# A two-layer sequence kernel on one core: who issues the first transfers, and where four small pieces of the start stand

## The chip, the cores and the metric

One core of a Trainium2 chip. The time is that of one execution on the device, in microseconds, from the first to the last instruction with what lies around them. The whole input lies in the chip's memory at the start and the whole output there at the end; the host only lays arrays out.

## The reference, cut to what matters

Two residual layers over x, 16 sequences of 256 steps with 512 channels each. The first is a causal convolution of 16 taps, one weight for each channel and tap. The taps are the rows of `cond`, which is also the first state of the second layer, a GRU:

```
x = x + conv(x, cond)                      # y[t] = sum over 16 taps, per channel
h = cond                                   # [16, 512]
for t in range(256):
    gi = x[t] @ W_ih + b_ih                # 512 -> 1536: r, z, n
    gh = h    @ W_hh + b_hh
    r = sigmoid(gi_r + gh_r);  z = sigmoid(gi_z + gh_z)
    n = tanh(gi_n + r * gh_n)
    h = (1 - z) * n + z * h
    out[t] = x[t] + h
```

All in float32.

## The kernel before

**Layout.** The 512 channels are 4 chunks (C = 4) over 128 partitions. The GRU's gates are computed in two halves, f = 0 and 1, each of two chunks (H = 2). The batch of 16 is the stationary side of a matmul: `recur(t, f, c)` (line 534) adds h's chunk c times W_hh to a PSUM tile `pg` for half f, in four column groups. `product(q)` (line 419) adds the input part x times W_ih for two steps at once, m = t // 2; q counts (m, f, c). A later scheme with formed weight differences (`group`, line 512) takes over from step 15.

**One step.** TensorE does the 64 recurrent matmuls of both halves; VectorE transposes the gates out of PSUM (lines 803, 807, 798), ScalarE does sigmoid and tanh (711, 713, 716), GpSimd z times h (408), VectorE the scans that give n's argument and h (815, 828). In the time between, TensorE does the products of coming steps.

**The convolution** is done in several ways. The first 16 steps: chunks 0 to 2 by VectorE as 60 multiply-adds (`first`, the first four steps, line 731, 12 of them; `rest`, line 741, 48 of them, the last 22 = LATE behind the two first transposes of the input gates), chunk 3 by TensorE with diagonal matrices that ScalarE writes (573, 696). Steps 16 to 47: chunk 0 by VectorE (`early`, line 775, 16 taps spread over the steps of EARLY), chunks 1 to 3 by TensorE as a product with a banded matrix (`turn`, line 565, in the step of ROUNDS), which reads windows of x (`xw`, line 241) and the band (`tz`, line 235, itself gathered from the taps that ScalarE has stored to memory, line 692). `spread` (789) brings the result to x1 in the step of TURNED. From step 48 on VectorE does all (759).

**The start, engine by engine**, each in program order:

- SP: cond, the first 16 steps of x (`xs`, 512 KB), four chunks of W_ih, four of W_hh (768 KB each, 6 KB for each partition), then waits for the third chunk of W_hh, then the window for `early`, the bands and windows step by step.
- ScalarE: b_ih, b_hh, then waits for GpSimd's `cpad` (the taps), stores them, writes 16 diagonals, copies the summed biases into six PSUM tiles (`seed`, 655), takes chunk 3's convolution out of PSUM, and copies a part of each chunk of W_hh (705).
- VectorE: two fills; waits for cond and copies it as h; waits for the biases, adds and transposes them (lines 840 to 851) to `bc`; waits for `xs`; then the 12 and 26 multiply-adds, the two transposes, the last 22.
- GpSimd: `eye`, `cpad`, fills; waits for `bc`; fills `tz` (321); then six small operations on `base`, `q21`, `q12`, `q22` and `delta` (322 to 327), needed first in step 11; then the loop over the steps.
- TensorE: zero products to open PSUM and six more (WARM); chunk 3's taps; the products of steps 0 to 3; waits for the two input transposes; then for each chunk c of W_hh the recurrent matmuls of step 0, behind chunk 0 the product (m = 2, c = 3), behind chunk 1 the product (m = 2, c = 0) (AHEAD), and behind chunk 0 two zero products (IDLE).

A DMA issued by SP runs on queue 1 and one by ScalarE on queue 10 of the same 16 DMA engines. In step 10 TensorE waits for the last tap of `early`, then opens the PSUM tile `stage` with a zero product (641), since `early` sums in that tile.

Of the kernel before, what the change touches and what calls it, by code (L numbers as in the profile page):

```python
# [10 lines left out]
J, C, D = 4, 4, 32  # L11
B, T, F = 16, 256, 512
# [7 lines left out]
TB = 16  # L20
# [10 lines left out]
FEW = 4  # L31
WARM = 6
LATE = 22
IDLE = {0: 2}
AHEAD = {0: 3, 1: 0}
M2 = T // 2
RZ, IN, END = CH * D, 3 * CH * D, 4 * CH * D
Q = 3
# [7 lines left out]
def build(nc, x, cond, w_ih, w_hh, b_ih, b_hh, out):  # L46
    assert J * D == P
    ctx = ExitStack()
    with ctx:
        def sb(name, shape, dt=F32):  # L50
            return ctx.enter_context(nc.sbuf_tensor(name, shape, dt))
# [4 lines left out]
        def sem(name):  # L56
            return ctx.enter_context(nc.semaphore(name))
# [5 lines left out]
        xs = sb("xs", [P, C, TB * B])  # L63
# [7 lines left out]
        cnd = sb("cnd", [P, C, B])  # L71
# [29 lines left out]
        s_cnd = sem("s_cnd")  # L101
        s_small = sem("s_small")
        s_xs = sem("s_xs")
# [17 lines left out]
        s_first = sem("s_first")  # L121
# [50 lines left out]
        def x1_of(c, a, b):  # L172

            return x1[:, c, a % KEEP * B:(a % KEEP + b - a) * B]

        def window(k):

            return xb[k % 2]

        def products(t):  # L180

            ahead = [(2 * H + f) * C + c for c in AHEAD.values() for f in range(H)]
            return [q for q in range(2 * H * C + C * t, 2 * H * C + C * (t + 1)) if q < H * C * M0 and q not in ahead]
# [10 lines left out]
            return range(total * min(max(t - a, 0), b - a) // (b - a), total * min(max(t + 1 - a, 0), b - a) // (b - a))  # L194


        ROUNDS = {1: 4, 2: 6, 3: 8}
        TURNED = {1: 5, 2: 7, 3: 9}
        EARLY = {1: 2, 2: 2, 3: 2, 4: 3, 6: 3, 8: 3, 10: 1}
        SPANS = [(a - W2 - 4, a - 4) for a, _ in LONG]  # L200
        BAND = {1: 0, 2: 2, 3: 4}
        WINDOWS = {1: (1, 3), 2: (3, 5), 3: (5, 7)}
# [2 lines left out]
        FIRST = [(lag, c) for lag in range(FEW) for c in range(C - 1)]  # L205
        REST = [(lag, c) for lag in range(K) for c in range(C - 1)]
# [22 lines left out]
        @block.sync  # L229
        def _(sp):  # L230
            def band(c, g):
                if c == BANDED[0] and g == 0:
                    sp.wait_ge(s_scr, 16)
                    sp.wait_ge(s_band, len(BANDED))
                sp.dma_start(tz[c][W2 * g:W2 * (g + 1), :, g * K:(g + 1) * K],  # L235
                             bass.AP(scratch, (g * C + c) * TAPS, [[1, W2], [G * C * TAPS, NQ], [1, K]])
                             ).then_inc(s_tz[c], 16)

            def load(c, q):
                i, g = divmod(q, G)  # L240
                sp.dma_start(xw[c][W2 * g:W2 * (g + 1), :, i, :],  # L241
                             x[:, c, TB * i * B:(TB * i + W2) * B].rearrange("(p e) (w b) -> e w p b", e=G, b=B)[g]
                             ).then_inc(s_xw[c], 16)

            def load_long(k, c, i):
                a, b = LONG[k]
                if i == c == k == 0:
                    sp.wait_ge(s_c3, 1)
                if i == c == 0 and k == 1:
                    sp.wait_ge(s_early, K)  # L250
                if i == 0 and k >= 2:
                    sp.wait_ge(s_long, LONGS * (k - 2) + W2 // C * 3 * (c + 1))
                n = (K - 1 + b - a) * B
                at, to = n * i // PIECES, n * (i + 1) // PIECES
                first = (a - K + 1) * B
                sp.dma_start(window(k)[:, c, at:to], x[:, c, first + at:first + to]).then_inc(s_xb[k][c], 16)

            def store(k, c):
                a, b = STORES[k]
                sp.wait_ge(s_o, b)  # L260
                sp.dma_start(out[:, c, a * B:b * B], x1_of(c, a, b)).then_inc(s_out[k], 16)

            sp.dma_start(cnd[:, :, :], cond).then_inc(s_cnd, 16)
            sp.dma_start(xs[:, :, :], x[:, :, 0:TB * B]).then_inc(s_xs, 16)
            for c in range(C):
                sp.dma_start(wih[:, c, :, :], w_ih[:, c, :, :]).then_inc(s_wih[c], 16)
            for c in range(C):
                sp.dma_start(whh[:, c, F:], w_hh[:, c, :]).then_inc(s_whh[c], 16)
            sp.wait_ge(s_whh[C - 2], 16)
            sp.dma_start(xb[1][:, 0, :], x[:, 0, B:(W2 + TB) * B]).then_inc(s_xe, 16)  # L270
            for t in range(T):
                sp.wait_ge(s_h[0], t + 1)
                for c in BANDED:
                    if t == BAND[c]:
                        for g in range(G):
                            band(c, g)
                    for q in share(2 * G, WINDOWS[c], t):
                        load(c, q)
                for k in range(len(LONG)):
                    for c in range(C):  # L280
                        for i in share(PIECES, arriving(k, c), t):
                            load_long(k, c, i)
                for k, (a, b) in enumerate(STORES[:NB - 1]):
                    for c in share(C, (b, b + C), t):
                        store(k, c)
                for k, (a, b) in enumerate(STORES[NB - 1:-1], NB - 1):
                    if b == t:
                        sp.wait_ge(s_o, b)
                        sp.dma_start(out[:, :, a * B:b * B], x1_of(slice(None), a, b)).then_inc(s_out[k], 16)
            a, b = STORES[-1]  # L290
            sp.wait_ge(s_o, b)
            sp.dma_start(out[:, :, a * B:b * B], x1_of(slice(None), a, b)).then_inc(s_out[len(STORES) - 1], 16)
            sp.wait_ge(s_o, T)
            sp.dma_start(out[:, 0:CH, (T - 1) * B:], x1_of(slice(0, CH), T - 1, T)).then_inc(s_fin[0], 16)
            sp.wait_ge(s_last, 1)
            sp.dma_start(out[:, CH:, (T - 1) * B:], x1_of(slice(CH, C), T - 1, T)).then_inc(s_fin[1], 16)
            for k in range(len(STORES)):
                sp.wait_ge(s_out[k], 16 * (C if k < NB - 1 else 1))
            for f in range(H):
                sp.wait_ge(s_fin[f], 16)  # L300

        @block.gpsimd
        def _(pool):
# [15 lines left out]
            pool.wait_ge(s_bc, H)  # L319
            for c in BANDED:  # L320
                pool.memset(tz[c][:, :, :], 0.0).then_inc(s_band, 1)
            pool.memset(base[:, END:], 0.0).then_inc(s_prep, 1)
            pool.tensor_copy(base[:, 0:END], bc[:, 0, :]).then_inc(s_prep, 1)
            pool.tensor_copy(q21[:, 0:RZ], bc[:, 0, 0:RZ]).then_inc(s_prep, 1)
# [93 lines left out]
        def _(pe):  # L418
            def product(q):

                m, f, c = q // (H * C), q // C % H, q % C
                if m < 2 and f == 0:
                    pe.wait_ge(s_wih[c], 16)
                if m < 2 and c < C - 1:
                    pe.wait_ge(s_first, len(FIRST))
                if c == (AHEAD[0] if m == 2 else 0):
                    pe.wait_ge(s_seed[f], m + 1)
                if FEW <= 2 * m and c == 0:
                    pe.wait_ge(s_first, len(FIRST) + len(REST))
                for j in range(J):  # L430
                    i = pe.matmul(pg[m % Q][f][D * j:D * (j + 1), RZ:END], x1_of(c, 2 * m, 2 * m + 2),  # L431
                                  wih[:, c, :, :].rearrange("p (g k) (j d) -> p j g k d", g=3, j=J)
                                  [:, j, :, f * CH:(f + 1) * CH],
                                  start=False, stop=True, skip_group_check=True)
                if c == (C - 2 if m == 2 else C - 1):
                    i.then_inc(s_gi[f], 1)
# [162 lines left out]
            for c in range(C):  # L599
# [3 lines left out]
                for f in range(H):  # L603
                    if c < C - 1:
                        recur(0, f, c)
                    else:
                        recur_first(f, c).then_inc(s_gh[f], 1)
                if c in AHEAD:
                    for f in range(H):
                        product((2 * H + f) * C + AHEAD[c])  # L610
                for _ in range(IDLE.get(c, 0)):
                    pe.matmul(pcv[0][:, :], zeros[:, 0:P], zeros[:, :], start=True, stop=True)
# [3 lines left out]
            for t in range(1, T):  # L616
                m = t // 2
# [14 lines left out]
                for c in range(C):  # L632
                    for q in products(t)[c:c + 1]:
                        product(q)
                    for e, at in ROUNDS.items():
                        for r in range(2 * c, 2 * c + 2):
# [10 lines left out]
        def _(act):  # L647
# [14 lines left out]
            def staged(t):  # L662
# [20 lines left out]
                if r == 3 and ready(g + 1):  # L683
# [2 lines left out]
                        act.wait_ge(s_prep, 6)  # L686
                    act.activation(stage[:, 0:END + IN], base[:, :], ACT.Copy).then_inc(s_base, 1)

            act.dma_start(bih[:, :], b_ih).then_inc(s_small, 16)
            act.dma_start(bhh[:, :], b_hh).then_inc(s_small, 16)  # L690
            act.wait_ge(s_cp, 3)
# [31 lines left out]
        def _(dve):  # L723
# [138 lines left out]
            for t in range(T):  # L862
# [12 lines left out]
                for k, i in tapped(t):  # L875
                    long(k, i, RIGHT)
                    long(k, i, WHOLE)
                for c, at in TURNED.items():
                    if t == at:
                        for q in range(NT):  # L880
                            spread(c, q)
                done = sum(n for at, n in EARLY.items() if at < t)
                for lag in range(done, done + EARLY.get(t, 0)):
                    early(lag)
# [35 lines left out]
```

## Time and profile before

| | |
|---|---|
| median of 3 runs | 993.23 us (992.36 to 993.47) |
| the profiled execution | 991.44 us |
| its span, first to last instruction | 989.7 us |
| TensorE busy | 976.7 us, 99% |
| VectorE busy | 892.7 us, 90% |
| ScalarE, GpSimd busy | 467.3 and 447.2 us |

Times in the profile count from the span's start. A matmul's busy time is modelled and overlaps its neighbours, so TensorE at 99% is not TensorE at its peak; the chain of waits says more. SPq and ACTq are the sequencers that issue DMAs.

### The profile page before, as it was taken

The page shows a single profiled execution, that of the slowest core. Times are in us where ns is not written, and L with a number is a line of the kernel's source. Part 1 is how long each engine was busy: PE and PEld are TensorE (multiplying, and loading weights), DVE is VectorE, ACT ScalarE, POOL GpSimd, SP SyncE. Part 2 cuts the span into 40 slices and gives each one's busy share as a digit, 9 for nine tenths or more (in the row PEclk, how much of TensorE's full clock was granted, in tenths as well). Part 3 has the DMA queues.
Part 4 walks back from the last instruction along what each step waited for, and adds up shares of the span by engine and source line. Part 5 has one row for each costly group of instructions (what it writes and reads, how often), then busy time and mean ns, then how long its engine had stood idle before and what let it go on. Part 6 is the DMA issues. An engine that isn't in the chain of part 4 may idle for free.

```text
span 989.7 us, 59526 instructions
## 1 busy us (share of the span) xinstructions
PE 976.7 (99%) x24833; PEld 784.4 (79%) x24833; DVE 892.7 (90%) x3075; ACT 467.3 (47%) x1996; POOL 447.2 (45%) x1222
## 2 busy tenths in 40 slices
PE   8999999999999999999999999999999999999996
PEld 6778887888888777788888888888888888888875
DVE  7879999999999999999999999999999988888565
ACT  5334444444444444444454444544444444444443
POOL 6544444444444444444444444444444444444442
PEclk9999999999999999999999999999999999999999
DMA  8721001010010101001010010101001010010000
GB/s 304 73 40 35 25 11 38 15 41 19 16 37 12 40 19 30 26 14 34 20 35 25 16 33 16 40 20 28 24 15 37 14 30 17 11 31 4 26 14 14
DMA packets 67006, 32.17 MB, mean 33 GB/s; under 512 B 44464, under 2 KB 65584, under 8 KB 66736
## 3 DMA queue, kind: packets, MB, share of 16 engines
q1 hardware_dynamic: 66304, 28.25, 11.1%
q8 instruction: 195, 3.19, 1.4%
q14 instruction: 75, 0.61, 0.2%
q10 hardware_dynamic: 432, 0.11, 0.0%
HBM read 19.86 MB, written 8.49 MB: 29 GB/s over the span
## 4 chain that ended last, share of the span: by engine, by line
PE 93%; SPq 1%; DVE 1%; issue 0%; DMA 0%; POOL 0%; ACT 0%; DVEq 0%; POOLq 0%
PE pg L537 65%; PE pcv L463 12%; PE pg L453 8%; PE pg L463 4%; PE pcv L453 4%; SPq L241 1%; SPq L235 0%; PE pg L431 0%; DMA xw<-x 0%; POOL nzh L408 0%; DVE hp L828 0%; ACT rz L711 0%; DVE gt L803 0%; DVE gn L807 0%; POOL wt L349 0%
## 5 line engine op out<-in xcount | busy, mean ns | idle before, releaser
L537 PE MATMUL pg<-whh,hp 128*32 128x192 f32 x16368 | 712.8, 326 | 4.5 <-DVE hp L828 4.1
L537 PEld LDWEIGHTS pg<-whh,hp 128*32 128x32 f32 x16368 | 527.7, 110 | 136.7 <-DVE hp L828 6.5
L759 DVE SCALAR_TENSOR_TENSOR pcv<-xb,cnd,pcv 128x256 f32<-128x256 f32 (+2 forms) x588 | 315.2, 536 | 6.9
L408 POOL TENSOR_TENSOR nzh<-rz,hp 128x32 f32<-128x32 f32 x512 | 158.0, 309 | 347.6 <-ACT rz L711 347.5
L711 ACT ACTIVATE rz<-gt 128x64 f32<-128x64 f32 x512 | 136.6, 267 | 342.3 <-DVE gt L803 314.6
L803 DVE STREAM_TRANSPOSE gt<-pg 128x128 f32<-128x128 f32 x512 | 162.3, 317 | 51.7 <-PE pg L537 42.0
L828 DVE TENSOR_TENSOR_SCAN hp<-zcp,nzh 128x96 f32<-128x96 f32 x512 | 173.3, 338 | 11.9 <-ACT nzh L716 9.4
L716 ACT ACTIVATE nzh<-an 128x32 f32<-128x32 f32 x512 | 121.4, 237 | 127.3 <-DVE an L815 127.3
L815 DVE TENSOR_TENSOR_SCAN an<-rz,gn 128x64 f32<-128x64 f32 x512 | 149.9, 293 | 18.9 <-issue 0.4
L463 PE MATMUL pcv<-wt,sx 128*32 128x192 f32 x2880 | 150.0, 326 | 0.0
L713 ACT ACTIVATE zcp<-gt 128x32 f32<-128x32 f32 x512 | 110.9, 217 | 0.0
L807 DVE STREAM_TRANSPOSE gn<-pg 128x64 f32<-128x64 f32 x512 | 107.4, 210 | 0.0
L463 PEld LDWEIGHTS pcv<-wt,sx 128*32 128x32 f32 x2880 | 90.7, 110 | 19.6
L660 ACT ACTIVATE pg<-q 128x256 f32<-128x256 f32 x180 | 68.9, 383 | 36.5 <-POOL q L393 36.5
L334 POOL TENSOR_TENSOR x<-x,hp 128x64 f32<-128x64 f32 x255 | 81.4, 319 | 0.2
L453 PE MATMUL pg<-wih,x 128*32 128x96 f32 (+1 forms) x1440 | 61.3, 273 | 0.0
L463 PE MATMUL pg<-wt,x 128*32 128x96 f32 (+1 forms) x1440 | 61.3, 273 | 0.0
L463 PEld LDWEIGHTS pg<-wt,x 128*32 128x32 f32 x1440 | 46.7, 110 | 11.7
L393 POOL TENSOR_TENSOR q<-e,delta 128x192 f32<-128x192 f32 x60 | 35.8, 596 | 40.7 <-DVE hp L828 40.7
L798 DVE STREAM_TRANSPOSE gn<-pg 128x64 f32<-128x64 f32 x256 | 53.6, 209 | 0.0
L453 PE MATMUL pcv<-wih,x 128*32 128x192 f32 x960 | 50.0, 326 | 0.0
L453 PE MATMUL pg<-wih,sx 128*32 128x192 f32 x960 | 50.0, 326 | 0.0
(81 smaller groups left out, 552.1 us busy)
## 6 DMA issues: line engine op xcount, KB each, us to landing
xb<-x SPq DMA_DIRECT2D x96, 94.0 KB, 2.0
out<-x SPq DMA_DIRECT2D x60, 128.0 KB, 1.8
wih<-w_ih SPq DMA_DIRECT2D x4, 768.0 KB, 8.0
whh<-w_hh SPq DMA_DIRECT2D x4, 768.0 KB, 14.1
xw<-x SPq DMA_DIRECT2D x24, 64.0 KB, 3.4
xb<-x SPq DMA_DIRECT2D x16, 62.0 KB, 1.9
tz<-taps SPq DMA_DIRECT2D x12, 64.0 KB, 3.3
xs<-x SPq DMA_DIRECT2D x1, 512.0 KB, 4.6
```

The source lines that it names most:

```text
L408: pool.tensor_tensor(nzh[:, f, ::2, :, 1], chunks(rz[:, f, 1, :, 1]), h_of(t - 1, slice(f * CH, (f + 1) * CH)), ALU.mult).then_inc(s_zh[f], 1)
L453: i = pe.matmul(out[D * j:D * (j + 1), at:at + IN].rearrange("p (g k d) -> p g k d", g=3, d=D)[:, :, part, :], left, wih[:, c, :, :].rearr ...
L463: i = pe.matmul(out[D * j:D * (j + 1), at:at + IN].rearrange("p (g k d) -> p g k d", g=3, d=D)[:, :, part, :], left, wt[:, n, c, :, :].rea ...
L537: i = pe.matmul(pg[t // 2 % Q][f][D * j:D * (j + 1), 0:IN], hp[:, t % 2, 2 * c + 1 - t % 2:2 * c + 3 - t % 2, :, 1].rearrange("p u b -> p ...
L711: act.activation(rz[:, f, :, :, 1].rearrange("p g (c b) -> p (g c) b", b=B), gt[:, f, :, u], ACT.Sigmoid).then_inc(s_rz[f], 1)
L713: act.activation(zcp[:, f, ::2, :, 1], gt[:, f, CH:, u], ACT.Sigmoid, scale=-1.0).then_inc(s_zc[f], 1)
L716: act.activation(nzh[:, f, ::2, :, 0], chunks(an[:, f, :, 1]), ACT.Tanh).then_inc(s_n[f], 1)
L759: dve.scalar_tensor_tensor(x1_of(c, a, b)[:, lo:hi] if lag == K - 1 else sums, xx[:, c, (K - 1 - lag) * B + lo:(K - 1 - lag) * B + hi], cn ...
L803: dve.transpose(gt[:, f, :, :].rearrange("p c r -> p (c r)"), pg[t // 2 % Q][f][:, RZ:IN]).then_inc(s_trz[f], 1)
L807: dve.transpose(gn[:, t // 2 % 2, :, f, :, :, 0].rearrange("p u c b -> p c u b"), pg[t // 2 % Q][f][:, 0:RZ]).then_inc(s_tn[f], 1)
L815: dve.tensor_tensor_scan(an[:, f].rearrange("p n s -> p (n s)"), rz[:, f, 0].rearrange("p n s -> p (n s)"), gn[:, t // 2 % 2, t % 2, f].re ...
L828: dve.tensor_tensor_scan(hp[:, (t + 1) % 2, a:a + n].rearrange("p c b s -> p (c b s)"), zcp[:, f, 0:n].rearrange("p c b s -> p (c b s)"), ...
```

## The change

Six edits. ScalarE issues cond, xs, b_ih, b_hh in this order at its start, and SP begins with the weights. The product (m = 2, c = 0) is no longer pulled into the prologue: it is done in the steps, and three zero products stand behind chunk 1. The wait for the seed follows it to the chunk that now comes first. Chunk 3's banded product goes from step 8 to 9, its `spread` from 9 to 10. The 16 taps of `early` end in step 9: two in step 8, two in 9. GpSimd's six small operations wait until VectorE has done all 60 multiply-adds of the first 16 steps.

```diff
-IDLE = {0: 2}
-AHEAD = {0: 3, 1: 0}
+IDLE = {0: 2, 1: 3}
+AHEAD = {0: 3}
...
-        ROUNDS = {1: 4, 2: 6, 3: 8}
-        TURNED = {1: 5, 2: 7, 3: 9}
-        EARLY = {1: 2, 2: 2, 3: 2, 4: 3, 6: 3, 8: 3, 10: 1}
+        ROUNDS = {1: 4, 2: 6, 3: 9}
+        TURNED = {1: 5, 2: 7, 3: 10}
+        EARLY = {1: 2, 2: 2, 3: 2, 4: 3, 6: 3, 8: 2, 9: 2}
...
-            sp.dma_start(cnd[:, :, :], cond).then_inc(s_cnd, 16)
-            sp.dma_start(xs[:, :, :], x[:, :, 0:TB * B]).then_inc(s_xs, 16)
             for c in range(C):
                 sp.dma_start(wih[:, c, :, :], w_ih[:, c, :, :]).then_inc(s_wih[c], 16)
...
             for c in BANDED:
                 pool.memset(tz[c][:, :, :], 0.0).then_inc(s_band, 1)
+            pool.wait_ge(s_first, len(FIRST) + len(REST))
             pool.memset(base[:, END:], 0.0).then_inc(s_prep, 1)
...
-                if c == (AHEAD[0] if m == 2 else 0):
+                if c == (C - 1 if m == 2 else 0):
                     pe.wait_ge(s_seed[f], m + 1)
...
+            act.dma_start(cnd[:, :, :], cond).then_inc(s_cnd, 16)
+            act.dma_start(xs[:, :, :], x[:, :, 0:TB * B]).then_inc(s_xs, 16)
             act.dma_start(bih[:, :], b_ih).then_inc(s_small, 16)
             act.dma_start(bhh[:, :], b_hh).then_inc(s_small, 16)
```

## Rows read from the trace of the kernel before

**Rows 1.** Page, part 4: the chain that ended last, shares by engine and line.

```profile
PE 93%; SPq 1%; DVE 1%; issue 0%; DMA 0%; POOL 0%; ACT 0%; DVEq 0%; POOLq 0%
PE pg L537 65%; PE pcv L463 12%; PE pg L453 8%; PE pg L463 4%; PE pcv L453 4%; SPq L241 1%; SPq L235 0%; PE pg L431 0%; DMA xw<-x 0%; POOL nzh L408 0%; DVE hp L828 0%; ACT rz L711 0%; DVE gt L803 0%; DVE gn L807 0%; POOL wt L349 0%
```

**Rows 2.** The chain in order of time, steps 8 to 10: start us, us, what.

```profile
54.07 3.37 DMA xw<-x
...
59.56 2.60 PE pg L537 x64
...
67.72 0.65 DVE x L775
```

**Rows 3.** Waits to 75 us: engine, tile, line, releaser: us, times, longest.

```profile
PE pcv L641 <- DVE x L775: 1.1, 1, 1.1
...
PEld pcv L565 <- DMA xw<-x: 0.8, 1, 0.8
```

**Rows 4.** Timeline, SP's DMA issues: start us, us, engine, line, operation, count.

```profile
0.80 0.40 SPq L263 DMA_DIRECT2D cnd<-cond  x1
1.25 0.67 SPq L264 DMA_DIRECT2D xs<-x  x1
1.97 2.52 SPq L266 DMA_DIRECT2D wih<-w_ih  x4
```

**Rows 5.** Timeline, ScalarE: the taps' store and the last part of W_hh.

```profile
3.31 0.33 ACTq L692 DMA_DIRECT2D taps<-cpad  x1
...
22.19 0.63 ACT L705 ACTIVATE whh<-whh 128x512 f32<-128x512 f32 x1 [1.18 <-DMA whh<-w_hh]
```

**Rows 6.** Timeline, VectorE to the first gate transpose; brackets: idle before, releaser.

```profile
2.98 0.17 DVE L841 COPY bcol<-bih 128x4 f32<-128x4 f32 x1
...
3.41 0.77 DVE L849 STREAM_TRANSPOSE bc<-bcol 128x256 f32<-128x256 f32 x2
5.89 0.68 DVE L731 SCALAR_TENSOR_TENSOR x<-xs,cnd 128x64 f32<-128x64 f32 x3 [1.71 <-DMA xs<-x]
...
16.17 0.51 DVE L798 STREAM_TRANSPOSE gn<-pg 128x64 f32<-128x64 f32 x2
16.59 4.78 DVE L741 SCALAR_TENSOR_TENSOR x<-xs,cnd,x 128x128 f32<-128x128 f32 x22
23.38 0.32 DVE L803 STREAM_TRANSPOSE gt<-pg 128x128 f32<-128x128 f32 x1 [2.01 <-PE pg L551]
```

**Rows 7.** Timeline, TensorE's matmuls to step 0.

```profile
3.79 2.77 PE L581 MATMUL pcv<-zeros 128*128 128x512 bf16 x6
...
16.82 0.83 PE L537 MATMUL pg<-whh,hp 128*32 128x192 f32 x16
...
18.24 0.60 PE L612 MATMUL pcv<-zeros 128*128 128x512 bf16 x2
...
21.43 0.86 PE L431 MATMUL pg<-wih,x 128*32 128x192 f32 x16 [1.32 <-DVE x L741]
22.10 0.83 PE L537 MATMUL pg<-whh,hp 128*32 128x192 f32 x16
```

**Rows 8.** Timeline, GpSimd's bias copies and its first product of step 0.

```profile
9.68 6.73 POOL L323 COPY base<-bc 128x256 f32<-128x256 f32 x1
...
16.98 0.63 POOL L327 TENSOR_TENSOR delta<-bc 128x192 f32<-128x192 f32 x1
24.13 0.31 POOL L408 TENSOR_TENSOR nzh<-rz,hp 128x32 f32<-128x32 f32 x1 [6.52 <-ACT rz L711]
```

**Rows 9.** DMA queues from 8.0 to 8.5 us: packets, MB, share of engines.

```profile
q1 hardware_dynamic: 30, 0.18, 94.5%
q10 hardware_dynamic: 30, 0.02, 13.5%
```

**Rows 10.** DMA issues to 75 us: line, count, KB, median us to landing.

```profile
xs<-x SPq DMA_DIRECT2D x1, 512.0 KB, 4.6
...
taps<-cpad ACTq DMA_DIRECT2D x1, 96.0 KB, 7.1
```

## The prediction

> **What bounds the kernel now.** I read the chain of waits first. TensorE carries 93% of it, and line 537 alone, the recurrence, has 65% [rows 1]. From the twelfth step on every step is TensorE work back to back, and the change touches nothing there. So it can act only in the first 75 us: the prologue up to the first gate transposes at 23.38 us [rows 6], and steps 8 to 11, where the chain leaves TensorE. There it goes through a landing of the banded windows and then through a VectorE tap [rows 2]. The wait table prices these: 0.8 us on the last landing before line 565, 1.1 us before the opening product of line 641 [rows 3]. In the prologue I read each engine's own row of the timeline. SP issues cond, then xs, then the eight weight transfers [rows 4]; ScalarE issues the two biases meanwhile, and they have landed by 2.98 us, when VectorE reads them [rows 6]. VectorE handles the biases before xs, then runs its taps without a gap from 5.89 to 21.37 us, with only the two input transposes in between, and then waits 2.01 us for TensorE [rows 6]. TensorE waits 1.3 us for those taps at 21.43 us [rows 7], and ScalarE receives the last weight chunk at 22.19 us [rows 5]. The prologue is a close race between weights, taps and TensorE; whichever comes 1 or 2 us late sets the end.
>
> **The late steps.** Chunk 3's product goes from step 8 to step 9. Its last window landed at 54.07 + 3.37 = 57.44 us [rows 2]; the recurrent matmuls of one step are 2.60 us [rows 2], so a step later TensorE reaches it over 2 us after that, and the 0.8 us wait goes [rows 3]; the same products cost the same one step later. What is late next is only TensorE itself. The early taps now finish in step 9 instead of step 10: as many in all, 16, but line 641 no longer waits 1.1 us for the last one [rows 2, 3]. The four transposes of chunk 3 take its place at the end of step 10, behind the h of that step, and nobody needs them before step 12. Together -1.9 us. SP's issue order for the windows is unchanged and follows h, so it moves along.
>
> **The moved product.** product(2, f, 0) leaves the prologue, and with it the 1.3 us wait [rows 7]; three zero products stand there instead, about 0.3 us each by the pair of 0.60 us [rows 7]. Two of its halves return in steps 0 and 1, 0.33 us each, where TensorE waits for h anyway: 0 to +0.3 us, taken as +0.1.
>
> **The DMA issues.** SP's first weight transfer moves from 1.97 to about 0.80 us, since 1.17 us of issuing go from ahead of it [rows 4]. ScalarE now issues cond at 0.8, xs at about 1.25 and the biases at about 1.9 and 2.4. The bytes are the same, so the last chunk can land at most some 1.2 us earlier. But xs used to be ahead of the weights on one queue. Now it is on the other queue, beside them. How the two queues share is the term that decides, and the trace has one case of it: the taps, 96 KB from ScalarE at 3.31 us [rows 5], took 7.1 us to land [rows 10] although nothing else was on their queue. In the half microsecond from 8.0 to 8.5 us each queue got exactly 30 packets, SP's with 0.18 MB, ScalarE's with 0.02 MB [rows 9]. So the engines take turns by packet, whatever its size: 16 engines x 0.5 us / 30 = 0.27 us for one small packet and the 6 KB weight packet that goes with it.
>
> xs is 128 rows x 4 runs of 1 KB, 32 packets for each engine. Each bias is 128 rows of 48 B, 8 for each engine. With three completion packets that makes 51 turns behind xs's first: 51 x 0.27 = 13.8 us, less about five turns that fall on SP's own completion packets (-1.3). Starting at about 2.7 us, xs lands near 12 and the biases near 15.5; cond's own turns and the late start that the taps show (their landing is 4 us over what 8 turns cost) can add 0 to 4 us. I take 16.5 us for the biases. Bounds: 3 us, if the small packets aren't held up at all; 20 us, when the weights run out.
>
> VectorE's program reads the biases before it waits for xs. From the first bias copy to the end of the transposes of line 849 is 1.2 us (2.98 to 4.18), so the first tap starts at 17.7 instead of 5.89 us: 11.8 us later. The two input transposes end at 28.5 instead of 16.68, the taps at 33.2 instead of 21.37 [rows 6]. TensorE may start the recurrence only after those transposes. From there it needs, by its old rows [rows 7]: 2.0 us to the end of the two zero products (16.82 to 18.84), 0.65 for chunk 1, 0.9 for three zero products, and 1.28 from 22.10 to the first transpose at 23.38. That is 4.85 us, so the first gates stand at 33.4 us: +10.0 us. The weights, in by about 21, no longer matter.
>
> **Bias copies behind the taps.** GpSimd's copy of the base took 6.73 us beside VectorE's taps; the operations from its end to the end of delta took 1.2 us (16.41 to 17.61) [rows 8]. Run alone after the last tap I put all six at 1.8 us, bounds 1.5 and 3. They end at 35.0 us. The first nzh product stood 0.75 us behind the first gate transpose (24.13 against 23.38) [rows 6, 8], so it would be due at 34.15 and is 0.85 us late; a little is absorbed by the tanh beside it. I take +0.7. If xs came as early as before, the same six would end at 23.2 us and cost nothing.
>
> **A rule against the row.** The row shows 30 to 30 packets at 0.18 to 0.02 MB [rows 9]. The Trainium skill, "DMA: Bandwidth & Descriptors", section "Queues, rings and completion order", says that each engine switches queues only at packet boundaries and that a packet may hold 9 to 17 descriptors; its section "SWDGE vs HWDGE vs iDMA" adds that a packet is preferably at most 4096 B. If that grouping held here, four 1 KB runs would go per turn, xs would need 8 turns, and a bias one. By the page xs would then land at about 6 us; by the row at 12. The row speaks against grouping, since grouped taps of 768 B would show several of them to one weight packet.
>
> **Sum.** +10.0 + 0.7 + 0.1 - 1.9 = +8.9 us. The profiled execution took 991.44 us for a span of 989.7 us; it would become 1000.3. The median of the runs is 993.23, 1.8 above the profiled one, so I forecast 1002.1, taken as 1002.
>
> **Rivals.**
> (A) The small packets get through, grouped as above or for another reason: xs and biases land by 6 to 7 us. For it: the biases, beside cond alone, were in by 2.98 us [rows 6]. Against it: the equal counts of [rows 9]. VectorE then starts at 7 to 8 us, 1.3 to 2 late, which its 2.01 us of waiting [rows 6] mostly covers, the last weights come about 1 us earlier, and the six GpSimd operations may cost up to 0.7. Prologue +0.4, late steps -1.9: 991.7, not slower. It decides as long as the biases land before about 8 us.
> (B) Sharing lies between: the biases land at 9 to 12 us. The shift of the first gates is then 2.6 to 5.6 us, plus 0.7, less 1.9: 994.6 to 997.6.
> (C) The forecast plus a slow TensorE. With xs at 12 us it idles 5 us and more twice, where its longest idle now is 1.3 us [rows 7]. The granted clock is listed as 1.0 throughout, the upper of its two levels (2.4 GHz), but six equal zero products took 2.77 us at 3.79 us, 0.46 each, and two took 0.60 at 18.24 [rows 7]. The 4.85 us path and step 0 behind it at up to twice the price: +2 to +6, so 1004 to 1008; I take 1006. The Trainium skill, "TensorE: Matmul & The Clock Gate", section "Part 1: The HAM clock gate", says an idle array falls from 2.4 to 1.2 GHz; no row here shows a fall after an idle stretch.
> (D) Everything on the new queue is as quick as alone, weights a full 1 us earlier, the six operations hidden: -0.5 - 1.9 = -2.4, so 990.8, faster.
>
> **Chances.** Forecast 0.46, its own range 998 to 1006; A 0.20; B 0.13; C 0.16; D 0.05. What a measurement of this kernel can tell from no change is 0.2%, 2 us: faster ends at 991.2, slower begins at 995.2. Faster: D and a third of A, 0.11. Same: the rest of A and the lower end of B, 0.17. Slower: 0.72. The range for 8 in 10 runs from 991.5, which keeps most of A, to 1006.5, the middle of C.
>
> **What would show it.** Time from issue to landing of xs (11 us, against 4.6 [rows 10]) and of the biases (14 us); equal packet counts on both queues from 3 to 15 us; VectorE's first tap near 17.7 us; first gate transpose near 33.4 us; the first nzh on line 408 directly behind GpSimd's delta. No wait ahead of lines 565 and 641. It is wrong if the first tap starts before 9 us; then A holds, and the change is worth what steps 8 to 10 give.

## The result and the profile after

The changed kernel takes 1003.03 us, median of 4 runs (1002.06 to 1003.24), against 992.8 us in the same comparison: ratio 1.0105, interval [1.0091, 1.012]. The forecast was 1002, with 991.5 to 1006.5. The span went from 989.7 to 1000.3 us.

VectorE's timeline shows the loss at a glance. It answers to [rows 6], with the same columns; lines have moved by one.

```profile
5.73 0.31 DVE L839 COPY hp<-cnd 128x32 f32<-128x32 f32 x2 [3.92 <-DMA cnd<-cond]
19.10 0.17 DVE L842 COPY bcol<-bih 128x4 f32<-128x4 f32 x1 [13.06 <-DMA bhh<-b_hh]
...
20.21 0.64 DVE L732 SCALAR_TENSOR_TENSOR x<-xs,cnd 128x64 f32<-128x64 f32 x3
...
30.35 0.38 DVE L799 STREAM_TRANSPOSE gn<-pg 128x64 f32<-128x64 f32 x2
30.65 4.43 DVE L742 SCALAR_TENSOR_TENSOR x<-xs,cnd,x 128x128 f32<-128x128 f32 x22
35.66 0.32 DVE L804 STREAM_TRANSPOSE gt<-pg 128x128 f32<-128x128 f32 x1 [0.58 <-PE pg L550]
```

The first tap starts at 20.21 instead of 5.89 us, 14.3 later; the first gate transpose at 35.66 instead of 23.38, 12.3 later. The 2.0 us between the two are 1.4 of the 2.01 us that VectorE used to wait there, and 0.6 that its taps and transposes took less (14.87 in place of 15.48 us from the first tap to the end of the last). The transfers that it waited for, from the DMA issues of the kernel after (KB each, us from issue to landing):

```profile
xs<-x ACTq DMA_DIRECT2D x1, 512.0 KB, 13.9
...
cnd<-cond ACTq DMA_DIRECT2D x1, 32.0 KB, 4.9
bih<-b_ih ACTq DMA_DIRECT2D x1, 6.0 KB, 15.2
bhh<-b_hh ACTq DMA_DIRECT2D x1, 6.0 KB, 16.2
```

A bias of 6 KB is under way for 16 us. The chain of waits of the same kernel now begins with that one transfer (start, us, what):

```profile
2.90 16.18 DMA bhh<-b_hh
```

The packets of both queues, as in [rows 9], in three windows of one microsecond (3 to 4, 8 to 9 and 14 to 15 us):

```profile
q1 hardware_dynamic: 54, 0.33, 82.5%
q10 hardware_dynamic: 55, 0.01, 6.2%
...
q1 hardware_dynamic: 48, 0.29, 77.8%
q10 hardware_dynamic: 45, 0.05, 18.3%
...
q1 hardware_dynamic: 73, 0.40, 96.9%
q10 hardware_dynamic: 72, 0.02, 7.9%
```

Packet for packet, whatever they weigh: nearly the same count on both, and some 6 to 33 times the bytes for the weights. In every microsecond from 6 to 19 us the two counts differ by 4 at most; only between 5 and 6 us, when cond is through and xs has hardly begun, are they 65 to 20. Equal counts show that both queues get the same number of packets; they do not show how many of one queue go in a row.

TensorE idles 9 us for xs, and 3 us for the two input transposes; its matmuls to step 1, answering to [rows 7]:

```profile
15.19 1.22 PE L572 MATMUL pcv<-xs,eye 128*128 128x256 f32 x2 [9.11 <-DMA xs<-x]
16.20 6.00 PE L572 MATMUL pcv<-xs,xb 128*128 128x256 f32 x32
22.41 5.41 PE L430 MATMUL pg<-wih,x 128*32 128x192 f32 x128 [0.21 <-issue]
30.84 0.86 PE L536 MATMUL pg<-whh,hp 128*32 128x192 f32 x16 [3.02 <-DVE gn L799]
...
37.70 2.81 PE L536 MATMUL pg<-whh,hp 128*32 128x192 f32 x64 [0.79 <-DVE hp L829]
```

The granted clock (the column before the last two) while it waits, by windows:

```profile
6.00:10.00 4.00, 0.08 (x1) 0.00 (x0) 0.04 (x1) 3.20 (x8) 1.13 (x6) 0.86 0.99 363
10.00:14.00 4.00, 0.00 (x0) 0.00 (x0) 0.00 (x0) 2.86 (x10) 0.00 (x0) 0.50 1.04 423
14.00:18.00 4.00, 2.81 (x7) 2.33 (x8) 0.00 (x0) 0.00 (x0) 0.00 (x0) 0.50 1.02 402
```

GpSimd's last bias operation and its first product of step 0, answering to [rows 8], and the scan that VectorE does meanwhile, in the changed kernel and before:

```profile
36.24 0.59 POOL L326 TENSOR_TENSOR delta<-bc 128x192 f32<-128x192 f32 x1
...
36.80 0.27 POOL L407 TENSOR_TENSOR nzh<-rz,hp 128x32 f32<-128x32 f32 x1
```

```profile
36.37 0.61 DVE L816 TENSOR_TENSOR_SCAN an<-rz,gn 128x64 f32<-128x64 f32 x1
```

```profile
24.09 0.29 DVE L815 TENSOR_TENSOR_SCAN an<-rz,gn 128x64 f32<-128x64 f32 x1
```

And the start of step 11, where line 640 is the opening product, with no wait in brackets any more (before, it stood at 68.42 behind 1.1 us of waiting, [rows 3]):

```profile
79.23 0.39 PE L640 MATMUL pcv<-zeros 128*128 128x512 bf16 x1
79.55 2.81 PE L536 MATMUL pg<-whh,hp 128*32 128x192 f32 x64
```

### The profile page after: what moved, and what is told of

The parts are those of the page before. It is cut to its first block, busy times and chain, and to the rows that moved or that the text cites. A ratio compares the mean times of both kernels' runs of the same rounds, so it can differ in the third digit from the quotient of the medians.

```text
span 1000.3 us, 59534 instructions
## 1 busy us (share of the span) xinstructions
PE 978.6 (98%) x24836; PEld 789.8 (79%) x24836; DVE 892.5 (89%) x3075; ACT 467.4 (47%) x1996; POOL 441.8 (44%) x1222
## 4 chain that ended last, share of the span: by engine, by line
PE 95%; DMA 2%; issue 1%; POOL 1%; DVE 1%; ACTq 0%; ACT 0%; POOLq 0%; DVEq 0%
PE pg L536 66%; PE pcv L462 12%; PE pg L452 8%; PE pg L462 4%; PE pcv L452 4%; DMA bhh<-b_hh 2%; PE pg L430 1%; POOL tz L319 1%; PE pcv L564 0%; DVE gt L804 0%; POOL nzh L407 0%; DVE hp L829 0%; ACT rz L712 0%; DVE gn L808 0%; ACTq L690 0%
## 6 DMA issues: line engine op xcount, KB each, us to landing
xs<-x ACTq DMA_DIRECT2D x1, 512.0 KB, 13.9
```

## The experiments

Each comparison has its own runs of the kernel before, 991.7 to 992.1 us, so ratios are the safe way to compare across them.

**1. Only the issue order back.** cond and xs again on SP ahead of the weights, the rest of the change kept.

```diff
-            act.dma_start(cnd[:, :, :], cond).then_inc(s_cnd, 16)
-            act.dma_start(xs[:, :, :], x[:, :, 0:TB * B]).then_inc(s_xs, 16)
+            sp.dma_start(cnd[:, :, :], cond).then_inc(s_cnd, 16)      # first on SP
+            sp.dma_start(xs[:, :, :], x[:, :, 0:TB * B]).then_inc(s_xs, 16)
```

> The changed kernel with cond and xs back on SP ahead of the weights; everything else of the change stays. My theory (xs and biases on ScalarE's queue take turns, packet by packet, with 6 KB weight packets, and all of the loss comes from that): xs lands again near 5.9 us, biases near 3, the first gate transpose is at 22.9 to 23.4 us, and the late steps keep their 1.8 us. So 990.5 to 991.5 us, against 992.8 before and 1003.0 changed. Rival 1 (the wait of GpSimd's copies costs too): 991.5 to 993. Rival 2 (the moved products or the late steps cost the time, and the issue order little): over 999.

Measured: 989.73 us, ratio 0.9979 [0.997, 0.9988]. The whole loss is gone and a gain of 2.0 us is left. The time is 0.8 us under the expected range, which was reckoned from 992.8 us for the kernel before; here that kernel has 991.74, and the gain of 2.0 lies within the 1.3 to 2.3 us that the range meant. Its VectorE timeline:

```profile
5.92 0.68 DVE L732 SCALAR_TENSOR_TENSOR x<-xs,cnd 128x64 f32<-128x64 f32 x3 [1.07 <-DMA xs<-x]
...
23.09 0.32 DVE L804 STREAM_TRANSPOSE gt<-pg 128x128 f32<-128x128 f32 x1 [2.27 <-PE pg L552]
```

**2. Only the issue order changed.** The same two lines moved the other way in the kernel before.

> The kernel before with the issue edit alone: ScalarE issues cond, xs, biases, SP the weights. My theory: VectorE's first tap near 20.2 us and its last tap near 35.1 as in the changed kernel. Here the product (m = 2, c = 0) stands in the prologue and waits for the last tap, and from there to the first gate transpose it was 1.95 us (21.43 to 23.38). So gates at 37.0 us, +13.6, none of the late gain except by chance: 1005 to 1007 us. Rival (the issue edit is not the cause): within 2 us of 992.8. If the waits for products had been what cost time in the changed kernel, this one would be faster than 1003.

Measured: 1006.64 us, ratio 1.0149 [1.0133, 1.0164], +14.9 us. VectorE's first tap is at 20.21 us as in the changed kernel, its first gate transpose at 37.47 (expected 37.0). So the issue order costs 15 us in a kernel that still has the product in the prologue, and moving that product gave back part of the loss: what is worth nothing in experiment 1 (compare 3) brings the gates 1.8 us earlier, 35.66 against 37.47, because TensorE otherwise waits for the last tap. The two kernels also differ in GpSimd's wait, by which the last tap ends 0.4 us earlier (35.08 against 35.47), so the 1.8 us are not shown for the product alone.

**3. Only the late steps.** ROUNDS, TURNED and EARLY of the change in the kernel before.

> The kernel before with the late steps alone: chunk 3's banded product in step 9, its result in step 10, early taps done in step 9. My theory: the waits ahead of the banded product (0.8) and of the opening product (1.1) go, and step 11 starts 1.8 us earlier than at 68.74: 990.7 to 991.3 us. Rival (VectorE becomes late in step 9 or 10, or the waits only move): 992.3 to 993.3.

Measured: 989.58 us, ratio 0.9978 [0.9969, 0.9988], -2.2 us (expected -1.5 to -2.1, from 992.8). It equals experiment 1, so with the old issue order the moved product and GpSimd's wait together are worth nothing that shows, and the gain is the late steps'.

**4. Biases first on ScalarE.** The order bih, bhh, cond, xs.

```diff
+            act.dma_start(bih[:, :], b_ih).then_inc(s_small, 16)
+            act.dma_start(bhh[:, :], b_hh).then_inc(s_small, 16)
             act.dma_start(cnd[:, :, :], cond).then_inc(s_cnd, 16)
             act.dma_start(xs[:, :, :], x[:, :, 0:TB * B]).then_inc(s_xs, 16)
-            act.dma_start(bih[:, :], b_ih).then_inc(s_small, 16)
-            act.dma_start(bhh[:, :], b_hh).then_inc(s_small, 16)
```

> The changed kernel with ScalarE issuing both biases first, then cond, then xs. My theory has two parts. The biases land by 6 us and VectorE's first tap starts when xs lands, near 15.5 us instead of 20.2. If TensorE's clock cost nothing, everything would then be 4.7 us earlier: 998.3. But TensorE has idled since 6 us and runs chunk 3's taps at a granted 0.5, done near 22.2 us as now; the 128 products then end near 27.8 and the two input transposes at 28.2 instead of 30.7. So 2.3 to 2.8 us gained: 1000.2 to 1000.7 us. Rival (the biases are not what VectorE waited for last): 1002.5 to 1003.5.

Measured: 1001.43 us, ratio 1.0098 [1.0083, 1.0113]. Under 1 us gained where I expected 2.5, a miss. Biases landed after 4.5 and 6.3 us, but cond after 7.8 and xs after 15.8, at 18.1 us:

```profile
18.09 0.68 DVE L732 SCALAR_TENSOR_TENSOR x<-xs,cnd 128x64 f32<-128x64 f32 x3 [7.16 <-DMA xs<-x]
...
29.12 0.50 DVE L799 STREAM_TRANSPOSE gn<-pg 128x64 f32<-128x64 f32 x2 [0.76 <-PE pg L430]
```

I had left the biases' own turns out of xs's time. In these two orders the last of the transfers lands at 18 to 19 us either way; the order only chose which one it is.

**5. W_ih in 1 KB runs.** Six transfers that each take two column blocks of all four chunks, in place of four of 6 KB runs; readers of W_ih wait for all six.

```diff
-            for c in range(C):
-                sp.dma_start(wih[:, c, :, :], w_ih[:, c, :, :]).then_inc(s_wih[c], 16)
+            for n in range(6):
+                sp.dma_start(wih[:, :, 2 * n:2 * n + 2, :], w_ih[:, :, 2 * n:2 * n + 2, :]).then_inc(s_wih[0], 16)
```

> The changed kernel with W_ih loaded by six transfers of 1 KB runs (two of the twelve column blocks of all four chunks each) in place of four of 6 KB runs; who reads W_ih waits for all six. Issue order and all the rest as in the changed kernel. My theory (one small packet waits for one packet of the other queue, so the price is set by the size of that packet): a turn shrinks from 0.27 us to about 0.1, xs lands at 6 to 7 us instead of 15.2, the biases at 7.5 to 9 instead of 19.1, the first tap is at 8.7 to 10 us, the first gate transpose near 24 to 25.5. 991 to 993.5 us where before is 991.7. Rival (the queues share by bytes, or ScalarE's queue is simply served late): packet size changes nothing, xs lands near 15 us, 1001 to 1003 us.

Measured: 993.76 us, ratio 1.0018 [1.0009, 1.0027]: 8.6 us of the loss gone (1.0105 less 1.0018, of 992), 0.3 outside the expected range. The steps came 0.7 to 1.7 us behind the latest expected: xs in at 7.7, the biases at 10.0, the first gate transpose at 27.17 us. Its landings:

```profile
xs<-x ACTq DMA_DIRECT2D x1, 512.0 KB, 6.5
...
bih<-b_ih ACTq DMA_DIRECT2D x1, 6.0 KB, 6.4
bhh<-b_hh ACTq DMA_DIRECT2D x1, 6.0 KB, 7.5
```

xs fell from 13.9 to 6.5 us and the biases from 15.2 and 16.2 to 6.4 and 7.5, with the same bytes and the same issue order. That rules out sharing by bytes: how W_ih's bytes are cut into packets sets the price. That it does so only through the length of a turn isn't shown. Here the counts are not equal: SP's and ScalarE's queues got 310 and 1 packets from 3 to 4 us, 144 and 440 from 4 to 6, 352 and 143 from 7 to 8, and SP was 7.14 us issuing W_ih's six transfers where it took 2.29 for four. Most of xs went while SP's queue moved little, so xs may have gained by more than shorter turns; why is open. What is left of the loss is the biases, in at 10.0 us and so a first tap at 11.14, and W_ih, which the 128 products now had to await until 15.46; they then took 7.09 in place of 5.41 us, at a granted clock of 0.84 and 0.73 in the windows from 14 to 22 us, and VectorE waited 0.34 us for them.

**6. xs back on SP, cond and biases on ScalarE.**

> The changed kernel with xs back on SP as its first transfer, then the weights; ScalarE issues cond and the biases. My theory: the small transfers are few and early, so they meet 1 KB packets only; xs lands some 0.4 us earlier than in the kernel with cond and xs on SP, 5.5 us, the weights too. That one was held by the last weights, so gates at 22.7 us instead of 23.1 and 0.2 to 0.4 us less: 989.3 to 989.6 where that one had 989.7. Rival (cond or the biases now get caught behind 6 KB packets and hold GpSimd's taps or VectorE): first tap after 7 us, 990 or more.

Measured: 992.57 us (991.05 to 994.05), ratio 1.0001 [0.9992, 1.001]. The rival came true. xs landed after 4.3 us, but b_hh, issued at 1.69 us in place of 1.25, met the weights, whose first transfer SP now issued at 1.56 in place of 1.97 us, and took 6.5 us, so the first tap was at 9.37 us. And the runs spread over 3 us. In the profiled one TensorE idled 3.01 us for the transposes and the granted clock fell (windows: us, busy of PE, PEld, DVE, ACT, POOL with counts, PEclk, DMA share, GB/s):

```profile
18.00:22.00 4.00, 2.01 (x28) 1.49 (x32) 4.00 (x18) 1.26 (x2) 0.00 (x0) 0.63 0.73 263
22.00:26.00 4.00, 4.00 (x33) 1.12 (x25) 2.23 (x13) 0.63 (x1) 1.69 (x6) 0.52 0.79 132
```

```profile
19.99 1.51 PE L537 MATMUL pg<-whh,hp 128*32 128x192 f32 x16 [3.01 <-DVE gn L799]
```

Sixteen matmuls take 1.51 us in place of 0.83 to 0.86.

**7. The same without GpSimd's wait.**

> The previous kernel without GpSimd's wait for the last tap, so its six small operations run beside VectorE's taps again. My theory: the base copy takes 4 to 7 us instead of 0.40 and VectorE's last 22 taps take 4.8 us instead of 4.4, but neither is on the path, since VectorE waits about 2 us for TensorE there: within 0.3 us of the previous kernel. Rival (the wait is worth something by itself): 0.4 us or more slower than the previous one.

Measured: 992.51 us (990.81 to 993.0), ratio 1.0 [0.9992, 1.0009], the same as 6. In its profiled execution the same idle time of 3.01 us stands and no fall: those 16 matmuls take 0.86 us and the span is 989.1 instead of 992.0.

**8. Experiment 4 with TensorE kept busy** by 66 zero products in place of 6.

> The kernel with the biases first on ScalarE's queue (1001.4 us where before was 991.7) with 66 zero products instead of 6 ahead of chunk 3's taps, which fill TensorE's idle time up to the landing of xs at 18.1 us. My theory: the granted clock stays at 1.0, chunk 3's taps take 4.6 us instead of 6.4, the 128 products start near 22.8 instead of 24.55 us, and the input transposes then wait for VectorE's taps, not TensorE: 28.3 to 28.5 instead of 29.1. So 0.6 to 0.9 us less, 1000.5 to 1000.9. Rival (the low clock cost nothing, VectorE's taps held it all): no change, 1001.2 to 1001.7. If the zero products run past 18.1 us they cost that time themselves.

Measured: 1000.72 us, ratio 1.0087 [1.0073, 1.01]; experiment 4 had 1.0098. The profile shows the expected steps: the 128 products at 23.65 instead of 24.55 us, the transposes without a wait at 28.39, the gates at 33.69 instead of 34.58. The times differ by 0.7 us as expected, but the two intervals overlap, so it is the trace that carries this.

**9. Experiment 6 with 13 zero products in the second idle stretch.**

```diff
+            for _ in range(13):
+                pe.matmul(pcv[0][:, :], zeros[:, 0:P], zeros[:, :], start=True, stop=True)
             pe.wait_ge(s_tin[0], 1)
```

> The kernel with xs on SP and cond and the biases on ScalarE (992.57 us, runs from 991.05 to 994.05) plus 13 zero products in TensorE's idle 3.0 us between the 128 products and the recurrence. In its profiled execution the granted clock fell to 0.63 and 0.52 there and step 0's first matmuls took 1.51 us in place of 0.86. My theory (the spread of 3 us is this fall, whenever it happens): no run above 991.8, median 991.0 to 991.5, granted clock 0.999 in all. Rival (the spread is something else): median and spread as without them.

Measured: 991.29 us, ten of eleven runs between 991.13 and 991.61 and one at 993.48, above the expected limit of 991.8; ratio 0.9994 [0.9985, 1.0003], where 6 had 1.0001. The median is 1.3 us lower, though the two intervals overlap; the narrow spread is what shows that the idle stretch made the scatter. The clock goes with it: in experiment 6 the four runs under 992 us have a mean granted clock of 0.999, the seven others 0.996 to 0.998, and the one slow run here has the lowest of its eleven, 0.998.

**10. The changed kernel without GpSimd's wait.**

> The changed kernel without GpSimd's wait for the last tap. There the first gate transpose to the start of step 1 was 2.04 us where it was 1.71 before, with the first nzh directly behind delta. My theory: those 0.33 us go, VectorE's last taps take 0.4 us more and still end before the gates; 0.2 to 0.4 us faster than the changed kernel, ratio to before 1.0101 to 1.0104. The forecast on record put 0.7 us on it. Rival (the wait also keeps VectorE quick, so without it the gates come later): slower than the changed kernel by 0.1 to 0.4 us.

Measured: 1002.63 us (1001.77 to 1003.73), ratio 1.0108 [1.0094, 1.0122]: inconclusive by time, since some of its executions, the profiled one too, have the clock fall before the recurrence. Its trace gives the term: from the first gate transpose (37.46) to step 1 (39.17) it is again 1.71 us, not 2.04. It also shows what the wait avoids. The base copy, which here runs beside the taps before the two transposes, and the last 22 taps, which have GpSimd's other four operations beside them; then the base copy in the changed kernel, with VectorE's taps over:

```profile
26.32 4.90 POOL L321 COPY base<-bc 128x256 f32<-128x256 f32 x1
```

```profile
31.17 4.82 DVE L741 SCALAR_TENSOR_TENSOR x<-xs,cnd,x 128x128 f32<-128x128 f32 x22
```

```profile
35.35 0.40 POOL L322 COPY base<-bc 128x256 f32<-128x256 f32 x1
```

4.90 us against 0.40 for the copy, and 4.82 against 4.43 us for the taps. The Trainium skill, "SBUF — State Buffer", section "SBUF: two separate sides", says that a VectorE operation with two SBUF inputs and a GpSimd operation that reads SBUF exclude each other for a whole instruction. The trace agrees: the taps read x and xs and leave no gap, and the copy ends at 31.22 us, 0.35 us after VectorE's transposes, which read PSUM, began at 30.87.

**11. The changed kernel with both idle stretches filled** (52 zero products ahead of the taps, 13 ahead of the recurrence).

> The changed kernel with TensorE kept busy by zero products in both idle stretches: 52 in place of 6 ahead of chunk 3's taps, 13 between the 128 products and the recurrence. My theory: VectorE's late first tap (20.2 us) holds everything, chunk 3's taps end at 19.8 instead of 22.2 and nobody gains, since the 128 products wait for the 12 first taps at 22.3 us. So 0 to 0.3 us faster than the changed kernel in the profile, up to 1 us in the median since in some executions the clock also falls in the second stretch. Rival (the low clock carries a large part of the 10 us): 3 us or more faster.

Measured: 1003.05 us, ratio 1.011 [1.0096, 1.0124]: nothing gained that shows. Its granted clock is 1.0 in all windows, where the changed kernel has 0.66 from 6 to 15 us and 0.71 from 15 to 22. TensorE then simply waits longer for VectorE's first taps:

```profile
22.65 5.41 PE L430 MATMUL pg<-wih,x 128*32 128x192 f32 x128 [2.08 <-DVE x L734]
```

## Why the prediction was right

**The deciding term was right: turns by packet.** Experiments 1 and 2 put the whole loss on the issue edit, in both directions, the packet counts of the changed kernel are equal from 6 to 19 us at very unequal bytes, and experiment 5 shows that the size of the other queue's packets sets the price, though not by turns alone. The row that gave it was one half microsecond of [rows 9], read as a rate for one packet instead of as a share of bandwidth.

**Its size was too small by 2.6 us.** xs was put near 12 us and the biases at 16.5; they came at 15.19 and 19.1. The 51 turns themselves were nearly right: 13.4 us, 9.5 from cond's landing (5.7) to that of xs for 33 turns and 3.9 to the biases for 18, where 12.5 were forecast. What failed is the start of 2.7 us with the line "cond's own turns and the late start ... can add 0 to 4 us", of which little was taken (2.7 and 12.5 make 15.2, not the stated 15.5, so 1.3 us in all). cond stood on the same starved queue: ScalarE's queue moved nothing before 2.5 us, cond's packets then took until 5.2, and the first of xs went after 5.5. cond landed after 4.9 us instead of 1.8, and everything behind it on the queue moved by 3.

**From the first tap to the gates it held.** 4.93 us from the end of the two transposes to the gates, against 4.85. The taps ended at 35.08, and TensorE no longer waited for them. So the gates came 12.3 us late, where the forecast had 10.0.

**GpSimd's six operations** took 1.7 us (1.8 forecast) and the first nzh did stand directly behind delta, but only 0.33 us reached step 1 (2.04 against 1.71), not 0.7, and by another path than the forecast's. The late nzh cost nothing: it ended at 37.07 us, before the tanh (37.02 + 0.23 = 37.25) that the next scan needs as well. The sigmoid was not late either (0.41 us behind the transpose in both). The delay is VectorE's first scan: beside GpSimd's delta (36.24 to 36.83 us) it took 0.61 in place of 0.29 us. In experiment 6 delta had ended before the gates, the same scan took 0.29 and step 1 came after 1.70 us; in experiment 9, the same kernel with 13 zero products, delta fell beside the scan, which took 0.60, and step 1 came after 2.03. Nothing that shows is left for the moved product's 0.1.

**The late steps** gave 1.8 us up to step 11 (+12.61 us at step 1's start, 37.70 against 25.09, and +10.81 at step 11's, 79.55 against 68.74), forecast 1.9; experiment 3 measures 2.2 by itself. The sum in the profile is 12.3 + 0.3 - 1.8 - 0.2 over the rest of the run = +10.6 us, against +8.9 forecast. That the time itself came nearer, 1003.03 us against 1002, is partly luck: the forecast added to 993.23 us for the kernel before, which has 992.8 in this comparison and 991.7 to 992.1 in the later ones.

**Rival C was half right.** The granted clock did fall while TensorE idled from 6 us on, to 0.50, its lower level of 1.2 GHz, and chunk 3's taps took 6.0 us in place of the 4.56 that they took in the kernel before. The Trainium skill, "TensorE: Matmul & The Clock Gate", section "Part 1: The HAM clock gate", says that an idle array falls from 2.4 to 1.2 GHz, and the trace agrees. I gave it 2 to 6 us; in the changed kernel's profile it cost nothing, because the taps ended at 22.2 us, just as VectorE finished the first 12 multiply-adds, and experiment 11 without it was no faster. The 4.85 us path stood at full clock in that profile. Where that path does meet the fall it is longer than 4.93 us by 2.7 in the trace of experiment 6 and by 1.3 in that of experiment 10. The unprofiled runs of the changed kernel may have met it too: those at 1003.22 and 1003.24 us have mean granted clocks of 0.993 and 0.991, those at 1002.06 and 1002.84 have 0.994; no trace shows it.

**The grouping by 4 KB**, which would have led to rival A, did not happen: 48 to 45 packets with 1 KB ones on ScalarE's queue. Had four of them gone for one weight packet, the counts would stand 1 to 4.

## What to carry to other kernels

Before moving a transfer to another engine's queue, count its packets and look at the size of the packets that it will run beside: here the price was about the number of small packets for each engine times the time of one large one, 0.2 to 0.3 us each, and a transfer of 6 KB took 16 us. What the computation needs first goes ahead of the bulk on the bulk's own queue, or so early that the bulk has not begun; in experiment 6 biases issued 0.4 us later and weights issued 0.4 us earlier were enough to lose it. And read an edit's parts apart: here 2 us of good scheduling were hidden under 12 us of starvation, and the kernel before with the late steps alone, 989.6 us, beats both.

## What had not been expected

- Reordering the starved queue hardly moved its end: experiment 4 moved the last bias from 19.1 to 7.5 us and xs from 15.2 to 18.1, and the time by less than 1 us.
- An idle stretch of 3.0 us before the recurrence brought the granted clock down in the trace of experiment 6 and not in that of experiment 7. The runs of one and the same kernel, experiment 6, look like both cases: 991.1, 992.6 and 994.1 us with mean granted clocks of 0.999, 0.998 to 0.997 and 0.996. A median of few runs can't be read without the clock beside it.
- With 1 KB packets on both queues (experiment 5) the 33 turns of xs took 5.2 us, about 4 less than the 9.5 beside 6 KB ones, and the biases' 18 turns 2.3 in place of 3.9; the counts of the two queues were then not equal. What decides which queue's packets are ready is open, as is why ScalarE's queue moved nothing before 2.5 us in the changed kernel, with cond issued at 0.81.
